# Indirect reads with rows of their own, an earlier start of the last stage's jobs, and a routing choice made in two pieces

## The reference

```python
x = x + tanh(g_xattn[0]) * L0_xattn(ln(x), ctx, ctx, ...)   # A: values mixed over time by a correlation
x = x + tanh(g_ffn[0])   * L0_ffn(ln(x), ...)               # B: one expert of 8 per token
x = x + tanh(g_xattn[1]) * L1_xattn(ln(x), ctx, ...)        # C: attention, 16 heads of 8
x = x + tanh(g_ffn[1])   * L1_ffn(ln(x), ...)               # D: two experts of 8 per token

# B
route = softmax(x @ router_w + router_b); e = argmax(route)
a, g = split(x @ w1[e]);  y = (silu(a) * g) @ w2[e] * max(route)
# D
h = int(x[:, 0] + x[:, 1]) mod 8;  sel = (h, h + 1 mod 8)
y = 0.5 * sum over e in sel of relu(x @ W1[e] + b1[e]) @ W2[e] + b2[e]
```

## Time and profile before

| | us |
|---|---|
| median of 3 runs | 358.47 (357.48 to 359.72) |
| the profiled execution | 358.9 |
| its span | 357.1 |
| TensorE busy in the span | 306.1 (86%) |
| VectorE, ScalarE, GpSimd busy | 195.1, 158.2, 163.3 |
| mean granted clock | 0.952 |

### The profile page before, as it was taken

The page is one execution under the profiler, slowest core; times in us unless marked ns, Lnnn a source line. Parts: engine busy times, 40 slices in busy tenths (PEclk is TensorE's granted clock), DMA queues, the critical chain, the costliest instruction groups (busy, mean ns, idle before and its releaser), DMA issues.

```text
span 357.1 us, 8461 instructions
## 1 busy us (share of the span) xinstructions
PE 306.1 (86%) x2870; PEld 250.3 (70%) x2882; DVE 195.1 (55%) x592; ACT 158.2 (44%) x335; POOL 163.3 (46%) x345
## 2 busy tenths in 40 slices
PE   8997995978998999977999999986585996969995
PEld 3657652978998999534677777753265996869895
DVE  7558757233433442465788878656713653435563
ACT  1253602111544552433867676872103663435462
POOL 8550403763665534234555464511470045655542
PEclk9999989896999999999999999999568999989999
DMA  7939992284212210446765552089543012222110
GB/s 209 352 87 372 332 259 74 72 187 111 67 58 67 60 39 31 125 106 171 144 157 148 157 129 60 6 270 289 194 90 16 2 32 59 53 45 53 38 31 25
DMA packets 35889, 42.63 MB, mean 119 GB/s; under 512 B 4868, under 2 KB 30511, under 8 KB 34687
## 3 DMA queue, kind: packets, MB, share of 16 engines
q1 hardware_dynamic: 28872, 31.79, 31.2%
q0 software_dynamic: 3664, 8.73, 10.5%
q10 hardware_dynamic: 3312, 1.58, 1.7%
HBM read 30.84 MB, written 10.96 MB: 117 GB/s over the span
## 4 chain that ended last, share of the span: by engine, by line
PE 60%; DVE 14%; another core or an unknown queue 7%; issue 7%; DMA 4%; ACT 3%; POOL 3%; DVEq 1%; SPq 0%; ACTq 0%; POOLq 0%
PE bank L1254 9%; PE pairB L1045 6%; PE pairA L1045 6%; PE bank L1054 5%; PE bank L1723 4%; PE pairB L1244 4%; PE pairA L1693 3%; PE pairA L1244 3%; PE pairB L1709 3%; PE pairB L344 2%; PE pairA L344 2%; DVE maxi L1793 1%; DMA x<-in_x 1%; PE bank L1741 1%
## 5 line engine op out<-in xcount | busy, mean ns | idle before, releaser
L1254 PE MATMUL bank<-wring,prob 128*128 x312 | 44.3, 287 | 11.8 <-DVE prob L1310 6.9
L1254 PEld LDWEIGHTS bank<-wring,prob 128*128 128x128 f32 x312 | 39.6, 199 | 14.1 <-issue 13.6
L1793 DVE TENSOR_REDUCE maxi<-pairA 128x8 f32<-128x1024 f32 x30 | 36.7, 1222 | 14.3 <-PE pairA L1693 12.9
L1765 ACT ACTIVATE prob<-pairB 128x1024 f32<-128x1024 f32 x30 | 30.7, 1024 | 14.5 <-PE pairB L1709 14.4
L1359 POOL DMA_INDIRECT out_x<-qs,inv_i x16 | 15.9, 996 | 45.5 <-DVE qs L1323 44.4
L1155 POOL DMA_INDIRECT back_d<-ysb,inv_i x23 | 22.7, 988 | 28.1 <-DVE ysb L1116 24.9
L1150 POOL DMA_INDIRECT qs<-rows_b_d,inv_i x23 | 22.4, 976 | 23.3 <-DVE inv_i L760 16.7
L300 POOL TENSOR_TENSOR lnv<-lnv,neg_half 128x4 f32<-128x4 f32 (+1 forms) x12 | 14.8, 1232 | 29.5 <-DVE lnv L295 29.5
L1122 DVE COPY xtT<-bank 128x128 f32<-128x128 f32 x23 | 6.7, 292 | 38.0 <-PE bank L1031 27.0
L1281 ACT ACTIVATE xn<-wring 128x516 f32 x37 | 23.4, 633 | 7.9 <-DVE job_i L850 7.4
L1323 DVE SCALAR_TENSOR_TENSOR qs<-bank,job,qs 128x128 f32 x39 | 13.6, 349 | 23.8 <-PE bank L1254 13.5
(11 more groups left out here) (327 smaller groups left out, 703.5 us busy)
## 6 DMA issues: line engine op xcount, KB each, us to landing
wring<-in_wts SPq DMA_DIRECT2D x8, 768.0 KB, 8.3
wring<-in_wts SPq DMA_DIRECT2D x8, 514.0 KB, 5.2
ks<-kparts_d SPq DMA_DIRECT2D x12, 192.0 KB
qs<-qparts_d SPq DMA_DIRECT2D x12, 192.0 KB
kparts_d<-parts SPq DMA_DIRECT2D x8, 192.0 KB, 2.6
qparts_d<-parts SPq DMA_DIRECT2D x8, 192.0 KB, 3.0
ctx_s<-kparts_d SPq DMA_DIRECT2D x6, 192.0 KB
ctxT<-qparts_d SPq DMA_DIRECT2D x6, 192.0 KB
```

The source lines that it names most:

```text
L1254: j = eng.matmul(bank[1 + i % 2][:, 0:D], act[:, i % 2, c_, :], down_weights(e, o), start=(c_ == 0), stop=(c_ == C1 - 1))
L1765: eng.activation(prob[:, at.half(5), :, :].rearrange("p h t -> p (h t)"), turned_in(at.unit(5))[:, :, :].rearrange("p a t -> p (a t)"), AC ...
L1793: eng.reduce_max(maxi[:, at.half(0), :], scores_in(at.unit(0))[:, :, :].rearrange("p a (h t) -> p (a h) t", t=T), AX).then_inc(s("mx"), 1)
```

## The change

1. `b2pair_d` gets 8 x 128 rows, a copy of each pair's row for each partition, and `b2_i` becomes pair x 128 + partition. The write moves from POOL's prologue to SP, behind the key loads in `early_keys`, and reads `b2a` with a repeat of 128. POOL waits for it ahead of the first b2 gather.
2. A third index `inv_i[:, 2]` gives an unused slot the token of its partition's number; stage B gathers with it from tile 6 on (`AHEAD`).
3. `route_d` ends with the tables of jobs. The transpose of `seg` and the product for the gate become functions that `experts_d` calls: TensorE runs transpose of tile 0, `seg_pe`, up(0), `gate_pe`, up(1), transpose of tile 1, then loads its registers, then down(0). Tile and expert of jobs 0 and 1 are constants. VectorE is ordered alike.
4. Warm matmuls: `WARM[7]` 3 to 12, `WARM[8]` 2 to 4, `WARM[9]` 4 to 13 and moved ahead of the slot sums; in `b_pe` three fillers go.
5. Routing B: logits of group 1 are made between the transposes of groups 2 and 3; the last group's go to another bank. VectorE makes the choice for twelve batches after group 2 and for four after group 3; the second one-hot and the shifted logits for the exponent come behind it.

```diff
-    WARM = (26, 14, 16, 10, 30, 12, 3, 3, 2, 4, 6, 2, 18)
+    WARM = (26, 14, 16, 10, 30, 12, 3, 12, 4, 13, 6, 2, 18)
-        b2pair_d = scratch("b2pair_d", (NE, D))
+        b2pair_d = scratch("b2pair_d", (NE * T, D))
@@ consts (POOL) and a_pool
-            eng.wait_ge(s("b2pair"), 3)
-            eng.dma_start(b2pair_d, b2a[:, :]).then_inc(s("b2pair_d"), 16)
-            eng.wait_ge(s("b2pair_d"), 16)
@@ route_b, dve
+                eng.scalar_tensor_tensor(inv_i[:, 2, :], inv[:, 1, :], part[:, :], inv[:, 3, :], ALU.mult, ALU.add)
@@ route_d, dve
-                eng.tensor_copy(b2_i[:, :], seg[:, :]).then_inc(s("b2_i"), 1)
+                eng.tensor_scalar(b2_i[:, :], seg[:, :], float(T), part[:, :], ALU.mult, ALU.add).then_inc(s("b2_i"), 1)
+            DV.append(dve)
+
+            def seg_dve(eng):
                 eng.wait_ge(s("job_sums"), 2)
                 eng.tensor_scalar(segT[:, :], segTp, back, None, ALU.subtract).then_inc(s("job_made"), 1)
+
+            def gate_dve(eng):
+                c = chain(eng, "dve")
                 eng.wait_ge(s("job_sums"), 3)
                 c.link(eng.tensor_tensor(away, of_job, iota_p[:, 0:NJ], ALU.subtract))
...
@@ route_d, pe2
+                warm(eng, bank[5], WARM[9])
                 eng.wait_ge(s("hotk"), 2)
...
                 warm(eng, bank[5], WARM[8])
+            PE.append(pe2)
+
+            def seg_pe(eng):
                 eng.wait_ge(s("job_made"), 2)
                 eng.transpose(segTp, seg[:, :], ident[:, :]).then_inc(s("job_sums"), 1)
+
+            def gate_pe(eng):
                 eng.wait_ge(s("job_made"), 3)
                 eng.matmul(of_job, segT[:, :], begun[:, 2, :], start=True, stop=True).then_inc(s("job_sums"), 1)
-                warm(eng, bank[5], WARM[9])
-            PE.append(pe2)
@@ b_pe
+        def logits_at(b, n=1):
+
+            at = bank[2] if b < NB - GB else bank[6]
+            return at[:, b * NE:(b + n) * NE]
...
             turned(1)
-            warm(eng, bank[4], B_WARM[1])
             logits(0)
             turned(2)
-            warm(eng, bank[4], B_WARM[2])
+            logits(1)
             turned(3)
-            for g in range(1, G):
-                i = logits(g)
-            i.then_inc(s("logit"), 1)
+            for g in range(2, G):
+                logits(g).then_inc(s("logit"), 1)
@@ b_dve
+            def chosen(k, lo, hi):
+                n = hi - lo
+                of = slice(lo, hi)
+                eng.wait_ge(s("logit"), k)
+                c.link(eng.tensor_tensor(logit[:, of, :], logits_at(lo, n).rearrange("p (b e) -> p b e", e=NE), bc(rb[:, :], 1, n), ALU.add))
+                c.link(eng.reduce_max(r16[:, 1, of], logit[:, of, :], AX))
+                c.link(eng.tensor_tensor(oh[:, of, :], logit[:, of, :], bc(r16[:, 1, of], 2, NE), ALU.is_equal))
+                c.link(eng.scalar_tensor_tensor(lw[:, 2, of, :], oh[:, of, :], -float(NE), bc(iota_e[:, :], 1, n), ALU.mult, ALU.add))
+                c.link(eng.tensor_reduce(r16[:, 2, of], lw[:, 2, of, :], AX, ALU.min))
+                return eng.scalar_tensor_tensor(ohb[:, of, :], bc(iota_e[:, :], 1, n), -float(NE), bc(r16[:, 2, of], 2, NE), ALU.add, ALU.is_equal)
+
+            eng.wait_ge(s("consts"), 1)
+            chosen(1, 0, NB - GB)
+            chosen(2, NB - GB, NB).then_inc(s("oh"), 1)
@@ experts_b, gather
-                                       in_offset=bass.IndirectOffsetOnAxis(ap=inv_i[:, 0, t.k:t.k + 1], axis=0)).then_inc(xt_in[t.x], 16)
+                                       in_offset=bass.IndirectOffsetOnAxis(ap=inv_i[:, 0 if t.k < AHEAD else 2, t.k:t.k + 1], axis=0)).then_inc(xt_in[t.x], 16)
@@ experts_d, pe
+                turn_over(eng, 0)
+                seg_pe(eng)
+                up(eng, 0, 0)
+                gate_pe(eng)
+                up(eng, 1, 0)
+                turn_over(eng, 1)
                 eng.wait_ge(s("te"), 2)
                 job_tiles = job_block(mybir.EngineType.PE, 0, 0)
-                expert = job_block(mybir.EngineType.PE, 1, 0)
-                turn_over(eng, 0)
-                for i in range(NI):
+                expert = [0, 1] + job_block(mybir.EngineType.PE, 1, 0)[2:]
+                down(eng, 0, expert[0])
+                for i in range(2, NI):
...
@@ experts_d, dve
-                eng.wait_ge(s("te"), 2)
+                xT(eng, 0)
+                seg_dve(eng)
+                relu_dve(eng, 0)
+                gate_dve(eng)
+                relu_dve(eng, 1)
+                xT(eng, 1)
                 job_tiles = job_block(mybir.EngineType.DVE, 0, 0)
...
@@ experts_d, pool
                 eng.wait_ge(s("b2_i"), 1)
+                eng.wait_ge(s("b2pair_d"), 16)
@@ early_keys (SP)
+            eng.wait_ge(s("b2pair"), 3)
+            eng.dma_start(b2pair_d.rearrange("(e p) d -> e p d", e=NE), bc(b2a[:, :], 1, T)).then_inc(s("b2pair_d"), 16)
```

More of the change, by code:

```diff
@@ L213, in build @@
         inv = sb("inv", [128, 4, KP])
-        inv_i = sb("inv_i", [128, 2, KP], i32)
+        inv_i = sb("inv_i", [128, 3, KP], i32)
         ends = sb("ends", [128, 4, NE])
@@ L861, in dve @@
                 c.link(eng.tensor_tensor(gate, low, wrap, ALU.mult))
-            DV.append(dve)
             def act(eng):
@@ L882, in pe2 @@
                 warm(eng, bank[5], WARM[8])
+            PE.append(pe2)
+            def seg_pe(eng):
                 eng.wait_ge(s("job_made"), 2)
                 eng.transpose(segTp, seg[:, :], ident[:, :]).then_inc(s("job_sums"), 1)
+            def gate_pe(eng):
                 eng.wait_ge(s("job_made"), 3)
                 eng.matmul(of_job, segT[:, :], begun[:, 2, :], start=True, stop=True).then_inc(s("job_sums"), 1)
-                warm(eng, bank[5], WARM[9])
-            PE.append(pe2)
-            return gate
+            return gate, (seg_dve, gate_dve), (seg_pe, gate_pe)
         def registers(engine, row, n):
@@ L950, in logits @@
                 for b in range(g * GB, (g + 1) * GB):
-                    i = eng.matmul(bank[2][:, b * NE:(b + 1) * NE], big[:, b, :], rw[:, :], start=True, stop=True)
+                    i = eng.matmul(logits_at(b), big[:, b, :], rw[:, :], start=True, stop=True)
                 return i
@@ L992, in b_dve @@
             c = chain(eng, "dve")
[L993 to L1003 removed]
+            def chosen(k, lo, hi):
[11 more added lines that the diff above has]
+            chosen(2, NB - GB, NB).then_inc(s("oh"), 1)
+            c.link(eng.scalar_tensor_tensor(oh[:, :, :], bc(iota_e[:, :], 1, NB), -float(NE), bc(r16[:, 2, :], 2, NE), ALU.add, ALU.is_equal))
+            eng.tensor_tensor(lw[:, 0, :, :], logit[:, :, :], bc(r16[:, 1, :], 2, NE), ALU.subtract).then_inc(s("shifted"), 1)
         DV.append(b_dve)
@@ L1190, in experts_b, with experts_d @@
             SP.append(sp_back)
-        def experts_d(wts, gate):
+        def experts_d(wts, gate, late_dve, late_pe):
+            seg_dve, gate_dve = late_dve
+            seg_pe, gate_pe = late_pe
             n = {k: s(f"{k}_d") for k in ("xTp", "xT", "h", "half", "act", "yp", "y", "ups")}
@@ L1217, in weights_in, with tile_of @@
                     wait(eng, n["ups"], i - 1)
+            def tile_of(buf, tau, lo):
+                if isinstance(tau, int):
+                    return buf[:, tau, lo:lo + D]
+                return buf[:, ds(tau, 1), lo:lo + D].rearrange("p a d -> p (a d)")
             def down_weights(e, o):
-                return wd[:, ds(e, 1), o:o + D].rearrange("p a d -> p (a d)")
+                return tile_of(wd, e, o)
             def job_block(engine, row, k):
@@ L1244, in up @@
                     j = eng.matmul(P[:, g_, o * T:(o + 1) * T], w[:, f * 128:(f + 1) * 128],
-                                   xT_all[:, ds(tau, 1), :].rearrange("p a t -> p (a t)"), start=True, stop=True)
+                                   tile_of(xT_all, tau, 0), start=True, stop=True)
                 j.then_inc(n["h"], 1)
@@ L1269, in pe @@
                         turn_over(eng, i // 2 + 1)
-                    if i >= 1:
-                        down(eng, i - 1, expert[i - 1])
+                    down(eng, i - 1, expert[i - 1])
                 down(eng, NI - 1, expert[NI - 1])
@@ L1330, in dve @@
             def dve(eng):
-                eng.wait_ge(s("te"), 2)
+                xT(eng, 0)
[4 more added lines that the diff above has]
+                xT(eng, 1)
                 job_tiles = job_block(mybir.EngineType.DVE, 0, 0)
-                xT(eng, 0)
-                for i in range(NI):
-                    relu_dve(eng, i)
+                for i in range(1, NI):
+                    if i > 1:
+                        relu_dve(eng, i)
                     if i % 2 == 0 and i // 2 + 1 < TT:
@@ L1896, in build @@
         DV.append(d_dve)
-        gate_d = route_d()
-        experts_d(A["wts1"], gate_d)
+        gate_d, late_dve, late_pe = route_d()
+        experts_d(A["wts1"], gate_d, late_dve, late_pe)
         emit()
```

9 lines of the change are left out of this document (removed).

## The result

| | kernel before | changed kernel |
|---|---|---|
| median, us | 359.7 (20 runs, 357.15 to 366.12) | 356.56 (20 runs, 350.53 to 362.44) |
| profiled execution, us | 358.9 (span 357.1, clock 0.952) | 354.42 (span 352.7, clock 0.974) |

The ratio is 0.987, 95% interval 0.9835 to 0.9905: 1.3%, or 4.7 us of 359.7, where 14 us were forecast. It compares the fast executions alone (7 of the changed kernel's 20, 18 of the other's); the medians of all 20 in the table lie 3.1 us apart, and that is how the two numbers fit together. 356.56 lies just above the forecast's range (337 to 356), and at the time of rival B (356: "the stall belongs to POOL's software DMAs, not to the rows").

What follows compares the result with a forecast made beforehand. TensorE idle or at 1.2 GHz bounds the kernel, with 18.6 us of last-stage stalls blamed mostly on shared b2 rows. 5.0 + 6.7 + 3.0 + 0.4 - 1.0 = 14.1 off 358.9 gave 344; 80% range 337 to 356.

Steps and rivals of the forecast that it cites:

- rival B: Last stage: the stall belongs to POOL's software DMAs, not the rows; gain 2.4 us, time 356, chance 0.20.
- Own rows, first group (5.0): Last stage, first four b2 gathers: own rows remove the 6.0 us gap between jobs 2 and 3; 5.0 us taken.
- later groups (6.7): Last stage, 12 later b2 gathers mixed with scatters and row gathers: 6.7 of 12.6 us of stall gained.
- 105 against 292 GB/s per unit of share: Last stage: b2 gathers alone against gathers of distinct rows, read as shared rows making b2 slow.
- The check the forecast itself named: Last stage: if b2 moves fast and the late pitch is still 2.2 us, rows were not the cause there.
- 6.4% idle with 13.5%: TensorE idle in stage B against the late last stage; by that ratio 0.47 of the later stall stays.
- Eight dense gathers, no delay: Start of last stage: eight distinct-row gathers, yet job 0's product releases ScalarE on time; counted against POOL's DMAs as cause.
- Two jobs ahead (3.0): Start of last stage: jobs 0 and 1 start early at full clock, job 2 up at 262.6 not 265.62; gain 3.0 us.
- It is kept through a stall: Last stage: the 3.0 us head start survives a stall, since POOL issues its gathers at the same times.
- Routing (0.4, or 1.2 if the clock stays): First routing: logits and fillers end some 0.4 us earlier; 1.2 us should the clock stay at 2.4.
- The 512 KB write (-1.0, 0 to 2.3): SP's b2 copy near 75 us slows the stretch from 76 to 88; loss 1.0 us, between 0 and 2.3.
- Rival E: Slower: the 512 KB write doubles the loss from 76 to 88 us, last-stage stalls stay; 362 to 368, chance 0.06.

Runs made afterwards that it cites:

- e1: Kernel before with only the own rows for b2 and the pads (items 1 and 2): ratio 1.004, median 357.26 us.
- e10: Changed kernel without the own rows, two jobs ahead and new routing kept: ratio 0.9906 to the kernel before, median 353.57 us.
- e9: Changed kernel itself, run again as yardstick on another chip: ratio 0.9967 to the kernel before, median 356.51 us.
- e16: Changed kernel without own rows, last stage's indirect DMAs paced, on a chip that stalls: ratio 0.9594 to the kernel before, 346.30 us.
- e12: Complete changed kernel with all GpSimd indirect DMAs of the last stage paced by the jobs: ratio 0.9599 to the kernel before, 343.65 us.
- e11: Changed kernel without the two jobs ahead and their warm matmuls: ratio 0.9981 to the kernel before, median 355.61 us.
- e2: Kernel before with only the two jobs ahead and their warm matmuls (items 3 and 4): ratio 1.0022, median 355.87 us.
- e17: Kernel before with only the pacing of the last stage's indirect DMAs, on a chip that stalls: ratio 0.9694, 348.66 us.
- e14: Kernel before with only the pacing of the last stage's indirect DMAs, on the chip without stalls: ratio 1.0052, 330.95 us.
- e13: Changed kernel without own rows, last stage's indirect DMAs paced, on the chip without stalls: ratio 0.9888 to the kernel before, 325.21 us.
- e3: Kernel before with only the first routing in 12 and 4 batches (item 5): ratio 0.9966, median 355.44 us.
- e6: Changed kernel with row gathers 8 to 15 moved right behind the first four b2 gathers: ratio 0.997 to the kernel before, 359.96 us.
- e4: Changed kernel without the 16 b2 gathers, SP loading four tiles once: ratio 0.9542 to the kernel before, 342.33 us.
- e8: Changed kernel with b2 gathers replaced by plain DMAs of the same 64 KB from GpSimd: ratio 0.9539 to the kernel before, 344.49 us.

## Why the prediction was wrong

- **Own rows, first group (5.0) and later groups (6.7): wrong, and 11.7 us of the miss.** Measured: a loss of 0 to 2 us (e1, e10 against e9, e16 against e12). Rival B, with a chance of 0.20, is what the experiments bear out. Only the first gap answered to them, and only without the early jobs (job 0 to 4 in 11.9 us in e1 and 12.7 in e11, against 15.0 before and 15.5 in the changed kernel); why, stays open. Two steps failed. One is the inference from the earlier trace rows, 105 against 292 GB/s per unit of share, to the stall: that b2 gathers move slowly was true, that TensorE waits for it was not. The check the forecast itself named was the right one, b2 fast and a late pitch still at 2.2 us. The other is how it set aside the stalls of stage B: it compared 6.4% idle with 13.5% and put the difference down to rows. Stage B has two indirect DMAs per 2.8 us tile, the last stage three per 3.7 us; density would explain that order too, which no run tested. What spoke for B could be read before: 0.95 us for a gather and 0.30 to the next, so three DMAs per tile fill GpSimd's time. The Trainium skill (page "DMA: Bandwidth & Descriptors", section "Anatomy of one DMA — SWDGE (gpsimd) path"), whose fit has no term for rows, would have given 0 for own rows; the runs agree on the time, though the software queue's share fell from 10.5 to 8.1%, which the fit has no term for.
- **"Eight dense gathers, no delay", the evidence against B.** A true row, and a trap: job 0's product came at the end of these gathers and was on time. In the changed kernel, where products run among the same eight gathers, the delay is there. Perhaps little was under way before that could be late; no run shows why the first eight delayed nothing.
- **Two jobs ahead (3.0): right in its first steps, not borne out in the sum.** Job 0 went up at 257.74 in e2 and at 256.0 in the changed kernel (257.7 forecast, and 1.4 of the difference is the earlier start of the stage), clock 1.00. The next step, job 2 up at 262.6, failed: the stall begins as soon as products run among dense gathers, 6.3 us earlier than before, and job 2 went up at 265.39. "It is kept through a stall" is undecided. In the two profiles job 38 is 4.4 us earlier, 1.4 of it the earlier stage, so 3.0 us are kept, as forecast; but own rows alone shorten the stage as much, both together no more, and by its median e2 gave 0, as e9 against e11 did. Where the stalls are mostly paced away, or absent, early jobs and routing together give 1.0% (e17 against e16, 3.6 us) and 1.6% (e14 against e13, 5.4 us), against 3.4 forecast.
- **Routing (0.4, or 1.2 if the clock stays): the size of the upper case, without its reason.** In the changed kernel's profile the clock from 41 to 50 us was 1.00 instead of 0.81, and the ranks began at 48.26 instead of 49.83; but e3 alone gave 1.2 us (0.3 to 2.1) with the clock at 0.81, e9 and e10 have 0.81 too, and e1, with the old routing, has 1.00. So by these traces the routing does not decide this clock, and that the size was right is in part luck.
- **The 512 KB write (-1.0, 0 to 2.3): right.** 1.6 us less work in 12 us (e9 against e10), and a stage B 1.2 us longer in the mean of the traces. Rival E's second stall did not come: the change was never slower.
- **Pads (0):** not measured apart.

With rows at 0, the sum is 3.0 + 1.2 - 1.0 = 3.2 us with the early jobs whole and 0.2 without them; measured were 1.2 to 4.7 by the series.

## What to carry to other kernels

Before blaming a slow transfer, ask who waits for it: a queue's poor GB/s and a stall in the same stretch are two facts, not one. Count how much of the issuing engine's time its DMAs fill (here 3 x 1.27 us against a period of 3.7), and try spacing them before remaking what they read. A head start gained in front of a stall must be priced with the stall moved forward, too; a change that is judged on one chip may have been judged on that chip's stalls; and a state seen in one trace, such as a clock of 1.00, should be looked up in the others before a change gets the credit.

## What the runs showed of the hardware

**Back-to-back indirect DMAs from GpSimd delay TensorE's results.** With them issued every 1.25 us without a pause, ScalarE and VectorE got a finished product 5.8 us late (changed kernel, ten issued by then) and ScalarE one 13.8 us late (e6, all twenty issued). At two per 3.7 us TensorE was busy 66.00 of 66.00 us (e4), and e12's runs of one to three with pauses between them left it busy 66.67 of 69. Data went on moving meanwhile (82 and 81 GB/s). In the changed kernel the other work went on too: TensorE began its next transpose and the down product of job 0 (258.42, 258.75), VectorE worked off a chain of four small steps (259.40 to 260.20), and GpSimd issued on time. What in the chip is held up is open, and so is why e8's plain DMA spares it; no run tried plain DMAs without a pause.

**It depends on the chip.** The same program, e14 and e17, 330.95 and 348.66 us. By stage (B, then C, then the jobs after the first three), first e14, then e17:

```profile
62.00:127.00 65.00, 64.04 (x577) 63.34 (x578) 27.67 (x69) 27.58 (x38) 43.41 (x49) 1.00 0.36 92
127.00:243.00 116.00, 100.42 (x1330) 71.58 (x1329) 77.42 (x207) 66.99 (x142) 48.67 (x197) 0.98 0.56 148
256.00:321.00 65.00, 64.67 (x579) 64.38 (x578) 40.74 (x134) 40.52 (x105) 37.29 (x39) 1.00 0.25 53
```

```profile
63.00:139.00 76.00, 67.51 (x569) 65.77 (x570) 28.03 (x69) 27.55 (x37) 42.66 (x48) 0.96 0.32 78
140.00:256.00 116.00, 98.16 (x1321) 70.79 (x1327) 77.75 (x209) 66.82 (x142) 49.07 (x198) 0.98 0.56 147
269.00:341.00 72.00, 68.27 (x586) 65.94 (x586) 39.55 (x138) 40.26 (x107) 37.88 (x39) 1.00 0.23 48
```

Stage C takes 116 us on both. Stage B takes 65 us on one and 76 on the other. The last stage's jobs take 65 and 72. So only the stages with GpSimd's indirect DMAs differ. For the kernel before it is 329.87 against 359.76 us: 30 us, which is about this stage B's 11.8 plus the 18.6 us of stalls that the forecast counted in the last stage. By this sum the stalls were counted rightly; their cause was not. Why one of the four chips of these groups is free of them no run tells, and the change itself was not run there.

Of the complete kernels, e12 and e16 (0.960 and 0.959) beat both kernels where the stalls are, and e16 also beats the kernel before on the chip without them (as e13, 0.989). Stage B, with two indirect DMAs per tile of 2.8 us and some 11 us of stalls, is the largest part that is left; pacing it was not tried.
